# A graph network kernel: node chunks padded to single tiles of 128 edges in place of pairs, one sum per tile, blank rows spread over 128 indices

## The reference, cut to what matters

```
# layer 0 (hyperbolic attention), edge[0] = src, edge[1] = dst
h      = mobius_matvec(weight, h)
dist   = sqdist(h[src], h[dst]);  edge_h = 1 / (1 + dist)
edge_e = exp(-leaky_relu(logmap0(edge_h)))          # one norm over all edges
out    = elu(segment_sum(edge_e * logmap0(h)[dst], src) / segment_sum(edge_e, src))
x      = x + proj(expmap0(out))
# layer 1 (message passing)
m      = bn_relu(concat(h[src], h[dst], attr) @ Wm1 + bm1)
m      = bn_relu(m @ Wm2 + bm2)                       # batch norms over all edges
aggr   = segment_sum(m, src)
x      = x + bn_relu(bn_relu(concat(h, aggr) @ Wu1 + bu1) @ Wu2 + bu2)
```

## Time and profile before

| | us |
|---|---|
| median of 3 runs (lowest, highest) | 14630.19 (14626.67, 14637.61) |
| span of the profiled execution | 14632.4 |
| sort, up to the first gather | 0 to 2887 |
| first gather stage with its last functions | 2887 to 7351 |
| weighted sums | 7392 to 8274 |
| second gather stage | 8445 to 12829 |
| statistics of the second product | 12860 to 13276 |
| plain sums | 13320 to 14514 |

### The profile page before, as it was taken

One profiled execution on the slowest core, in us unless ns is written; L12 is line 12 of the kernel. 1 busy time (PEld: TensorE's weight loads), 2 busy tenths in 40 slices (PEclk: granted clock), 3 DMA queues, 4 the chain that ended last, 5 costly groups with the idle time before them and its releaser, 6 DMA issues. The chain is left out here.

```text
span 14632.4 us, 190137 instructions
## 1 busy us (share of the span) xinstructions
PE 6029.0 (41%) x50077; PEld 4977.9 (34%) x50078; DVE 8187.7 (56%) x17597; ACT 4342.3 (30%) x8364; POOL 9920.3 (68%) x10588
## 2 busy tenths in 40 slices
PE   3555555411111111111179633333333333288998
PEld 3555545411111111111078522222222222136997
DVE  6999999733343334343288844444444444367776
ACT  1888888700000000000079500000000000054334
POOL 0666666677777777777567467777777777604774
PEclk6777777755555555555589866666666666699999
DMA  2000000133333333333634332333333333574332
GB/s 67 9 9 9 9 9 9 26 88 88 88 87 88 88 88 87 88 87 88 66 124 152 93 80 81 81 81 81 81 81 81 81 82 83 67 239 139 106 106 78
DMA packets 1142542, 1160.65 MB, mean 79 GB/s; under 512 B 688977, under 2 KB 832977, under 8 KB 1142226
## 3 DMA queue, kind: packets, MB, share of 16 engines
q1 hardware_dynamic: 845842, 680.39, 16.6%
q0 software_dynamic: 235008, 248.13, 10.8%
q10 hardware_dynamic: 61632, 231.44, 4.0%
HBM read 872.56 MB, written 286.75 MB: 79 GB/s over the span
## 5 line engine op out<-in xcount | busy, mean ns | idle before, releaser
L1606 POOL DMA_INDIRECT big<-b_d,big x3424 | 3279.4, 958 | 1238.8 <-issue 980.1
L1092 POOL DMA_INDIRECT big<-h_d,big x3424 | 3308.5, 966 | 1061.7 <-issue 989.6
L1146 PE MATMUL ps<-big 128*128 x3424 | 653.2, 371 | 3788.7 <-PEq L147 3784.8
L1146 PEld LDWEIGHTS ps<-big 128*128 128x128 bf16 x3424 | 500.7, 164 | 3940.9 <-issue 3940.9
L1680 PE MATMUL ps<-big 128*128 x3424 | 565.6, 316 | 2902.3 <-PEq L147 2902.2
L1177 DVE TENSOR_TENSOR HA<-big 128x1024 f32<-128x1024 f32 x214 | 262.2, 1225 | 2528.0 <-DVEq L147 2526.6
L1680 PEld LDWEIGHTS ps<-big 128*128 128x128 bf16 x3424 | 409.3, 156 | 3219.4 <-issue 3219.3
L1929 POOL TENSOR_SCALAR big<-iota_f,big 128x128 f32<-128x128 f32 x1498 | 877.7, 609 | 847.6 <-DMA big<-rec_d 534.3
L1719 DVE TENSOR_TENSOR big<-ps,big 128x1024 f32<-128x1024 f32 x214 | 262.0, 1224 | 2024.2 <-DVEq L147 2024.2
L781 ACT ACTIVATE big<-big 128x512 bf16<-128x512 bf16 x1984 | 1228.9, 708 | 280.4 <-ACTq L147 280.4
L1100 ACT ACTIVATE big<-big 128x16 int32<-128x16 f32 x214 | 49.3, 230 | 4237.4 <-ACTq L147 4237.4
(11 more groups left out here) (405 smaller groups left out, 14622.3 us busy)
## 6 DMA issues: line engine op xcount, KB each, us to landing
big<-e_d SPq DMA_DIRECT2D x428, 512.0 KB, 3.2
rows_d<-big ACTq DMA_DIRECT2D x214, 544.0 KB, 2.8
big<-rows_d SPq DMA_DIRECT2D x214, 544.0 KB, 3.3
HA<-slots_d SPq DMA_DIRECT2D x214, 512.0 KB, 3.7
big<-slots_d SPq DMA_DIRECT2D x214, 512.0 KB, 4.5
e_d<-big ACTq DMA_DIRECT2D x214, 512.0 KB
big<-rec_d SPq DMA_DIRECT2D x860, 64.0 KB, 3.0
big<-h_d,big POOLq DMA_INDIRECT x3424
```

Of the source, the lines that this page charges most:

```text
L1092: gp.indirect_dma_start(G[g][:, t * ROW:(t + 1) * ROW], None, h0_d, bass.IndirectOffsetOnAxis(idx[g][:, t:t + 1], 0)).then_inc(gath[g], 16)
L1146: m = t.matmul(XS[h][:, n, 0:3 * D + 3], OT3[g % 2][:, o, :], T0[:, ds(chunks[o // 2] * TW, 3 * D + 3)], start=True, stop=True)
L1606: gp.indirect_dma_start(G[g][:, t * D:(t + 1) * D], None, b_d, bass.IndirectOffsetOnAxis(idx[g % 2][:, t:t + 1], 0)).then_inc(gath[g], 16)
```

## The change

A chunk now takes any number of tiles: counts are rounded up to 128 edges. `NTILES` = (412500 + 98 x 134) // 128 + 1 = 3326, 208 blocks, 3328 tiles. Each tile has its own chunk number: `ids` is twice as long, `chunks_of` loads 16 registers per block in place of 8. TensorE no longer accumulates two tiles; `add_sums` adds 16 results per block in place of 8. One more tile per block goes from VectorE to GpSimd in both sum stages: `POOL0` 4 to 5 (`ACT0` 9 to 10, so ScalarE keeps five and VectorE has six), `POOL1` 7 to 8 (VectorE eight). The filler record's `dst` is N plus (slot & 127) in place of N, so a blank tile gathers 128 different zero rows. 208 is 4 x 51 + 4, so all loops run 51 times over four blocks and then four blocks (`Q4`, `TAIL`), where they ran 53 times and then two.

```diff
-NPAIRS = (E + NCH * (2 * P - 1 + 7)) // (2 * P) + 1
-NBLK = -(-2 * NPAIRS // TB)
+NTILES = (E + NCH * (P - 1 + 7)) // P + 1
+NBLK = -(-NTILES // TB)
 NBLK += NBLK % 2
-TCOL = -(-NPR // P)
+Q4 = (NBLK - 1) // 4
+TAIL = NBLK - 4 * Q4
+TCOL = -(-NT // P)
...
-                ids[0:1, ds(t, 8)], engines=[eng.engine], min_val=0, max_val=NC - 1,
+                ids[0:1, ds(t, TB)], engines=[eng.engine], min_val=0, max_val=NC - 1,
...
+                gp.iota(blank_i, [[1, TB]], base=0, channel_multiplier=TB).then_inc(s_ip, 1)
...
-                v.memset(blank3[:, :, 1], float(N)).then_inc(s_bl, 1)
+                v.wait_ge(s_ip, 2)
+                v.tensor_scalar(blank_i, blank_i, P - 1, None, ALU.bitwise_and).then_inc(s_bl, 1)
+                v.wait_ge(s_bl, 3)
+                v.tensor_scalar(blank3[:, :, 1], blank_i, float(N), None, ALU.add).then_inc(s_bl, 1)
...
-                link(v.tensor_scalar(tot_i, ps[:, 0:NC], float(2 * P - 1 + L - 1), None, ALU.add))
-                link(v.tensor_scalar(tot_i, tot_i, 8, 1, ALU.logical_shift_right, ALU.logical_shift_left))
+                link(v.tensor_scalar(tot_i, ps[:, 0:NC], float(P - 1 + L - 1), None, ALU.add))
+                link(v.tensor_scalar(tot_i, tot_i, 7, None, ALU.logical_shift_right))
...
-        PARTS = (0, 16, 32, 44, NBLK // 4)
+        PARTS = (0, 16, 32, 44, Q4)
...
-                                         T0[:, ds(chunks[o // 2] * TW, 3 * D + 3)], start=True, stop=True)
+                                         T0[:, ds(chunks[o] * TW, 3 * D + 3)], start=True, stop=True)
...
-            chunks = chunks_of(v, k * (TB // 2))
-            for n in range(TB // 2):
-                if n % (TB // 4) == 0:
-                    hold(v, "v", q.mm[b], i * 2 + (q.mm_start + 1 + n // (TB // 4)))
+            chunks = chunks_of(v, k * TB)
+            for n in range(TB):
+                if n % (TB // 2) == 0:
+                    hold(v, "v", q.mm[b], i * 2 + (q.mm_start + 1 + n // (TB // 2)))
                 if n >= 2:
                     v.wait_ge(q.add, n - 1)
                 o = (q.AG2 if n % 2 else AG)[:, ds(chunks[n] * width, width)]
-                c0 = base + n // (TB // 4) * 512 + n % (TB // 4) * stride
+                c0 = base + n * stride
                 v.tensor_tensor(o, o, ps[:, c0:c0 + width], ALU.add).then_inc(q.add, 1)
...
-        POOL0, ACT0 = 4, 9
+        POOL0, ACT0 = 5, 10
...
-                        o = b * 2048 + n // 2 * P
+                        o = b * 2048 + n * P
                         m = t.matmul(ps[:, o:o + P], O4[g][:, n * P:(n + 1) * P],
-                                     G0[g][:, n * ROW:n * ROW + P], start=(n % 2 == 0), stop=(n % 2 == 1))
+                                     G0[g][:, n * ROW:n * ROW + P], start=True, stop=True)
...
-        POOL1 = 7
+        POOL1 = 8
...
-                        o = AGS[b] + n // (TB // 2) * 512 + n // 2 % (TB // 4) * D
+                        o = AGS[b] + n * D
                         m = t.matmul(ps[:, o:o + D], u1.O[b][:, n * P:(n + 1) * P],
-                                     MSG[b][:, n * D:(n + 1) * D], start=(n % 2 == 0), stop=(n % 2 == 1))
+                                     MSG[b][:, n * D:(n + 1) * D], start=True, stop=True)
```

More of the change, by code:

```diff
@@ L46 @@
 MAXNORM = 1.0 - 0.004
-assert COLS == NRB * RB and NCH == NIT * CPI
+assert COLS == NRB * RB and NCH == NIT * CPI and N + P <= NROW
 def build(nc, x, src, dst, attr, w0t, wm1, bm1, gm1, betm1, wm2, bm2, gm2, betm2,
@@ L104, in build @@
         blank3 = blank.rearrange("p (t w) -> p t w", w=REC)
+        blank_i = big[:, BIG - P - TB:BIG - P].bitcast(I32)
         top = [0]
@@ L187, in _ @@
                 v.tensor_copy(ident_b[:, :], ident[:, :]).then_inc(s_c, 1)
-                v.wait_ge(s_ip, 1)
+                v.wait_ge(s_ip, 2)
                 v.tensor_copy(iota_p[:, :], iota_pi[:, :]).then_inc(s_c, 1)
@@ L803, in _ @@
                                  base=0, pattern=[[1, GJ], [-1, GJ]], channel_multiplier=0).then_inc(s_pool, 1)
-                gp.iota(tgrid_i, [[2, TCOL]], base=0, channel_multiplier=2 * TCOL).then_inc(s_pool, 1)
+                gp.iota(tgrid_i, [[1, TCOL]], base=0, channel_multiplier=TCOL).then_inc(s_pool, 1)
                 for b in range(2):
@@ L1024, in each_block @@
                     part(q)
-            for g in range(NBLK % 4):
-                body(g, NBLK // 4, NBLK - NBLK % 4 + g, g == NBLK % 4 - 1, True)
+            for g in range(TAIL):
+                body(g, Q4, Q4 * 4 + g, g == TAIL - 1, True)
             if part is not None:
@@ L1074, in _ @@
                 each_block(sp, spread)
-                for g in range(NBLK % 4, 4):
+                for g in range(TAIL, 4):
                     sp.wait_ge(rec_in[g], 16)
-                for g in range(NBLK % 4):
+                for g in range(TAIL):
                     sp.wait_ge(kept[g], 16)
@@ L1127, in _ @@
                             store(g, PARTS[q + 1], PARTS[q + 1] * 4 + g)
-                for k in range(NBLK // 4 * 4 - 4, NBLK):
+                for k in range(Q4 * 4 - 4, NBLK):
                     store(k % 4, k // 4, k, k + 3 < NBLK)
@@ L1140, in step @@
                     consume(t, ot_rdy)
-                    chunks = chunks_of(t, k * (TB // 2))
+                    chunks = chunks_of(t, k * TB)
                     for h in range(2):
@@ L1275, in add_sums @@
                 o = (q.AG2 if n % 2 else AG)[:, ds(chunks[n] * width, width)]
-                c0 = base + n // (TB // 4) * 512 + n % (TB // 4) * stride
+                c0 = base + n * stride
                 v.tensor_tensor(o, o, ps[:, c0:c0 + width], ALU.add).then_inc(q.add, 1)
-            v.wait_ge(q.add, TB // 2)
-            v.sem_inc(q.add, -(TB // 2))
+            v.wait_ge(q.add, TB)
+            v.sem_inc(q.add, -TB)
             v.sem_inc(q.freed[b], 1)
@@ L1300, in each_block @@
         def each_block(eng, body):
-            with eng.Fori(0, NBLK // 4) as i:
+            with eng.Fori(0, Q4) as i:
                 for g in range(4):
                     body(g, i)
-            for g in range(NBLK % 4):
-                body(g, NBLK // 4)
+            for g in range(TAIL):
+                body(g, Q4)
         def weighted_onehots(eng, who, g, i, tiles):
@@ L1349, in _ @@
                     load(g, 0)
-                with sp.Fori(1, NBLK // 4) as i:
+                with sp.Fori(1, Q4) as i:
                     for g in range(4):
                         load(g, i)
-                for g in range(NBLK % 4):
-                    load(g, NBLK // 4)
+                for g in range(TAIL):
+                    load(g, Q4)
             @block.vector
@@ L1367, in _ @@
                 weighted_onehots(v, "v", 0, 0, range(ACT0, TB))
-                with v.Fori(0, NBLK // 4) as i:
+                with v.Fori(0, Q4) as i:
                     for g in range(4):
                         block_of(g, i)
-                for g in range(NBLK % 4):
-                    block_of(g, NBLK // 4, last=(g == NBLK % 4 - 1))
+                for g in range(TAIL):
+                    block_of(g, Q4, last=(g == TAIL - 1))
             @block.tensor
@@ L1564, in every_block @@
                 body(g, 0, g, g == 0)
-            with eng.Fori(1, NBLK // 4) as i:
+            with eng.Fori(1, Q4) as i:
                 for g in range(4):
                     body(g, i, i * 4 + g)
-            for g in range(NBLK % 4):
-                body(g, NBLK // 4, NBLK - NBLK % 4 + g, False, g == NBLK % 4 - 1, True)
+            for g in range(TAIL):
+                body(g, Q4, Q4 * 4 + g, False, g == TAIL - 1, True)
         with nc.Block() as block:
@@ L1633, in step @@
                     a.sem_inc(g_rdy[g], 1)
-                    if not end:
+                    if not end or k + 2 < NBLK:
                         indices((g + 2) % 4)
@@ L1680, in step @@
                             m = t.matmul(XST[q % 2][:, n // 2, n % 2, :], OT3[g % 2][:, o, :],
-                                         T1[:, ds(chunks[o // 2] * (3 * D), 3 * D)], start=True, stop=True)
+                                         T1[:, ds(chunks[o] * (3 * D), 3 * D)], start=True, stop=True)
                         m.then_inc(xs_rdy[q % 2], 1)
```

1 line of the change is left out of this document (removed).

## The result

The changed kernel takes 14761.01 us (median of 4 runs, 14754.83 to 14769.9), the kernel before 14633.6 beside it (14626.67 to 14637.61). The ratio is 1.0087, 95% interval [1.0073, 1.0101].

A forecast was written before the change was run, and what follows sets the result against it. No engine bound the kernel throughout: GpSimd's gathers, VectorE in the weighted sums, TensorE in the plain sums. Terms -195 - 168 - 4 - 12 + 3 + 228 + 204 = +56 us gave 14686 us, range 14605 to 14770.

The forecast's parts named there:

- Six blocks fewer and no queue: Both gather stages: -195 and -168 us, each 121 for six blocks, the rest (74 and 47) for the queue at the end.
- The weighted sums: VectorE drops one one-hot, gains eight adds and becomes the bound: 5.33 us per block in place of 4.12, +228 us.
- I take nothing: Register loads of sixteen numbers in place of eight: no added time; at most 0.6 us more uncovered in the weighted sums.
- Rival B: Register load doubles, some 0.4 us uncovered per block of the weighted sums: +83 us, so 14769; chance eight per cent.
- The plain sums: VectorE with sixteen adds and eight one-hots takes 6.69 us per block in place of 5.55: +204 us.
- TensorE's 5.55 no longer sets the pace: Plain sums: TensorE's 5.55 us per block stops being the bound, as VectorE needs 6.69.
- TensorE named as releaser of VectorE: Sign of being wrong, in either sum stage: VectorE found waiting for TensorE; no size given.
- The statistics: Second product's statistics: six blocks fewer at 1.94 us per block, -12 us.
- The start: Chunk list before the first supertile: 26 columns, not 14, so 12 more VectorE instructions at 0.24 us each, +3 us.
- Rival A: Adds in both sum stages run at the unwaited pace: 241 us less, so 14445, faster than before; chance eight per cent.
- The forecast's own range: Whole kernel: 14615 to 14745 us, from the bounds of the pair step and of the idle time, given 66%.
- the remaining 6%: Chance left beside the forecast and its rivals, split evenly between a little faster and no change.

The follow-up runs named there:

- spread_alone: Kernel before, with only the blank records changed to name rows N to N+127 in turn; 214 blocks and pair sums stay: 14504.82 us, ratio 0.9915.
- adds_alone: Kernel before, each tile multiplied and added by itself, one-hots split as in the change; 214 blocks, pair layout, 8-number loads, blank rows N: 15139.26 us, one run.
- pe_busy: Changed kernel, TensorE multiplying each block's first tile of the plain sums five times in place of once: 14723.97 us, ratio 1.0064.
- three_sums: Changed kernel with three accumulators in both sum stages, not two, add n waiting for add n-3: 14513.06 us, ratio 0.992.

## Why the prediction was right, and where it was off

- *Six blocks fewer and no queue*, -363 forecast for both gather stages, with the -4 of the distance functions -367: -382 measured between the same marks. Right, and spread_alone shows the one-row delay by itself (132 us where 121 were estimated).
- *The weighted sums*, +228 forecast, +256 measured. The block without the longer load is right to 0.01 us, 5.34 in adds_alone against 5.33, by two small errors that cancel: the adds last 3.09 for the forecast 3.05, and the first one begins 1.62 us after the first one-hot, with 1.63 forecast, while the idle time stayed at 0.65. The step that failed is "I take nothing" for the register loads: eight numbers more take 1.100 - 0.597 = 0.50 us, 0.063 each, and 0.126 us of it per block came uncovered. Rival B had the mechanism and three times its size. That the measured 14761 lies near B's 14769 is chance: B's mechanism gave 26 of its 83 us, and other causes the rest.
- *The plain sums*, +204 forecast, +234 measured. "TensorE's 5.55 no longer sets the pace" is right for the mean. It left out that TensorE, now waiting for ScalarE, ran 33 stretches at half clock, in which its products came late for VectorE. That is 35 us, by pe_busy; without it the stage lies 7 below the forecast. TensorE named as releaser of VectorE was one of the prediction's own signs of being wrong, and here it shows.
- *The statistics*, -12 forecast, +8 measured: "six blocks fewer" at the old 1.94 us each. The loop's place cost 20 us.
- *The start*, +3 forecast for the chunk list and measured there as well; 5.8 of the other 6.5 us arise in the sort's loop, whose branch went from 0.120 to 0.218 us in each of 60 passes. That it is the place here too was not tried.
- *Rival A*, 8%: the pair step stayed at 0.38. The Trainium skill, VectorE: DVE Perf Modes, section The DRAIN you can't avoid, says of its eight copies that the semaphore costs nothing extra. For these adds that holds in three_sums, where each waits for the one three before, and not in the changed kernel, where it waits for the one two before: 0.155 against 0.19 us per add.
- *The range and the chances.* The forecast's own range of 14615 to 14745 is not what its bounds add up to: with +211 and +165 the sum is 14630, with +269 and +259 it is 14782. The measured time lies outside the first and inside the second. And half of the remaining 6% is 3 points, where 4 are added.

## What to carry to other kernels

Take a change apart before taking it whole: here one half (spread the index of blank records) is worth 0.85% by itself, and the other half (no padding to pairs) saves twelve blocks of gathers and pays for them with eight more dependent adds per block on the engine that already set the pace of one sum stage and was next in line in the other. When the bound moves from TensorE to another engine, price TensorE's matmuls at both clock levels wherever the new bound waits for them; and before explaining a change of some tens of us in code that was not touched, look at the time of each loop's branch. A chain of short adds into alternating accumulators wants one accumulator more than it looks: three in place of two brought an add from 0.19 to 0.155 us.

## What was not expected of the hardware

- Gathers in which all 128 indices name one row: 29.9 us per block where 128 neighbouring rows take 20.1, with the DMA engines at 0.81 busy for 49 GB/s.
- A load of chunk numbers into VectorE's registers: 0.597 us for 8, 1.100 for 16. The Trainium skill, Runtime: NRT & Kernel Launch, section Instruction fetch mechanics, has about 200 ns per register; these rows have 75 per register for 8, and 63 for each further one.
- A loop's branch on VectorE takes 0.11 to 0.26 us to the next instruction according to where the loop lies; two instructions ahead of it change a stage of 423 us by 20.
- Four more matmuls per block on TensorE made the kernel 37 us faster.
